# The second norm of a two-layer attention and experts kernel: its root by a power on GpSimd, its shift stored ahead, four pairs of rows loaded beside the experts

## The chip, the cores and the metric

One core of a Trainium2 chip runs the whole program in one launch. The metric is the device time of that launch in microseconds (us), a median over several runs.

## The reference

The input is x of 16 batches x 256 tokens x 256 features. Four units follow one another, each adding to x: an attention over a context (unit 0), self-attention with a top-2 mixture of eight small experts (unit 1), an attention over context and x jointly (unit 2, "joint"), and a full block (unit 3). Only the end of unit 3 and its sum with x matter here:

```python
h = layernorm(x + o, g1, b1)                    # o: causal attention
w = top2_shares(softmax(h @ wg))
h1 = gelu(einsum('bsd,edf->ebsf', h, w1) + bb1)
y = einsum('ebsf,efd->ebsd', h1, w2) + bb2
moe = einsum('ebsd,bse->bsd', y, w)
block = layernorm(h + moe, g2, b2)              # rsqrt(v + 1e-5) * g2 + b2
x = x + tanh(g_ffn[1]) * block
```

The x of the last line is the x after unit 2. With g = tanh(g_ffn[1]), the result is x + g*b2 + (normalised rows) * (g*g2).

## The kernel before

Four phases run one after the other, with a barrier of all engines between the blocks of each.

**Attention phase** (`attention_phase`). 64 jobs (unit, batch), in order of unit, flow through an order of steps that a planner (`orders`) writes out once, from the costs in `STAGES` and the needs in `job_steps`. Each engine, and the SP queue of DMAs, walks its own list `ORDER[engine]` strictly in order. A step of the SP list that waits for a semaphore holds all DMAs behind it, and a step of GpSimd (POOL) that waits holds all GpSimd work behind it. In unit 2, PROJ (PE, then DVE at L1251) completes x in a buffer `xs` (ring of seven); STOREX (L801) writes it to the DRAM tensor `x3`. Rings of three `o` buffers hold the heads' outputs. LNP (L1052, L1054) is the root of the norms in this phase: on GpSimd, an addition of EPS and a power of -0.5, both of 128x2 elements.

**Routing** (`route`) sorts the 8192 (token, choice) rows by expert, on DVE and PE at half clock, while SP and ScalarE load 17 MB of expert weights. **Experts** (`run_experts`) first has a block in which only SP acts (some semaphore counts and the wait for the weights, L1515 to L1522), then a block of 71 tiles of 128 rows: GpSimd gathers the rows of `h_normed` by an indirect DMA (L1535), PE turns them (L1571) and multiplies, GpSimd scatters the results into `expert_rows`, called `y_d` (L1543).

**The last stage** (`combine`) takes two batches at a time: 8 pairs, in a ring of 4 sets of buffers, as a hardware loop of two turns. Per pair SP loads h (512 KB), x (512 KB) and the two experts' rows y (1 MB) (L1718 to L1720). GpSimd adds b2 to x (L1731), when all three loads of the pair are there. DVE adds the experts' rows to h by their shares (L1777, eight instructions), takes mean and variance (L467, L470), the root by a guess in integers and three Newton steps (L439 to L452, twelve instructions of 128x4), and the shift (L1781). ScalarE normalises (L1751, four instructions); DVE multiplies by g2 and adds x (`add_residual`, L1766 and L1769), one pair behind; ScalarE issues two stores of 256 KB (L1743). The order on DVE is:

```python
for q in ring:
    ...                       # rows, moments, root, shift of pair q
    if q:
        add_residual(q - 1)
add_residual(RING - 1)
```

A block ahead of it loads g2 and b2 and multiplies them by g (L1696 to L1707).

Of the kernel before, what the change touches and what calls it, by code (L numbers as in the profile page):

```python
# [6 lines left out]
F32 = mybir.dt.float32  # L7
BF16 = mybir.dt.bfloat16
I32 = mybir.dt.int32
# [28 lines left out]
NEWTON = 3  # L38
# [36 lines left out]
def kv_at(u, b, src=0):  # L75
# [14 lines left out]
    "BPROJ": [("pool", 1.27)],  # L90
# [37 lines left out]
def heads_read(u, b):  # L128

    return [("FIN" if u < 2 else "PROJ", u, b, 0)] if u < 3 else [("HT", u, b, 0), ("STOREX", u, b, 0)]  # L130


def job_steps(u, b):
# [36 lines left out]
    x = add("LOADX", 0, ("STOREX", u - 1, b, 0) if u else None, (("STOREX" if old[0] < 3 else "PROJ"), *old, 0) if old else None)  # L170
# [184 lines left out]
BPROJ_AT = counted(of_kind("pool", "BPROJ"))  # L355
HNS_AT = counted(of_kind("dve", "HNS"))
# [38 lines left out]

class Chain:
# [36 lines left out]
RSQRT_GUESS = 0x5F3759DF  # L433
COMBINE_STEPS = 120


def root_guess(dve, s, var, out, v):

    s.done(dve.tensor_scalar(v, var, EPS, None, ALU.add))  # L439
    s.wait()  # L440
    s.done(dve.tensor_scalar(out.bitcast(I32), v.bitcast(I32), 1, None, ALU.logical_shift_right))  # L441
    s.wait()
    s.done(dve.tensor_scalar(out.bitcast(I32), out.bitcast(I32), -1.0, float(RSQRT_GUESS), ALU.mult, ALU.add))  # L443


def root_step(dve, s, out, v, w):

    s.done(dve.tensor_tensor(w, out, out, ALU.mult))  # L448
    s.wait()
    s.done(dve.scalar_tensor_tensor(out=w, in0=w, scalar=-0.5, in1=v, op0=ALU.mult, op1=ALU.mult))  # L450
    s.wait()
    s.done(dve.scalar_tensor_tensor(out=out, in0=w, scalar=1.5, in1=out, op0=ALU.add, op1=ALU.mult))  # L452


def inverse_root(dve, s, var, out, v, w):

    root_guess(dve, s, var, out, v)
    s.wait()
    for _ in range(NEWTON):
        root_step(dve, s, out, v, w)  # L460
        s.wait()


def norm_moments(dve, s, src, stats, mv, rstd, root_v, root_w, n):

    for t in range(n):
        s.done(dve.bn_stats(stats[:, t, :], src[:, t, :]))  # L467
    s.wait_alone()
    for t in range(n):
# [1342 lines left out]
```

## Time and profile before

| | us |
|---|---|
| median of 3 runs (2614.16 to 2621.49) | 2621.05 |
| the profiled execution's own time | 2617.61 |
| its span in the profile | 2615.9 |

The times in the rows are us from the start of the span. The span lies in the profiled execution's own time; 1.7 us lie around it. Over the whole span PE is busy 87%, DVE 64%, ScalarE 52%, GpSimd 37%, but these are averages over the four phases: after 2499 us PE does nothing at all. A change in one phase has to be read from that phase's rows.

### The profile page before, as it was taken

The numbers are of one execution on the slowest core, as the hardware profiler recorded it, in microseconds if no ns is written. First come the engines' busy times: TensorE is split into PE (matmuls) and PEld (weight loads), VectorE is DVE, ScalarE is ACT, GpSimd is POOL, SyncE is SP. The second block draws the span as 40 slices with busy tenths as digits, with TensorE's granted clock in tenths as the row PEclk, the third lists the DMA queues.
The fourth block names the chain that finished last, engine by engine and source line by source line (L and its number), as shares of the span: only waits on it lengthen the run. The fifth ranks groups of instructions, "written<-read, shape, count | busy, mean of one in ns | idle before, by whom it ended". The sixth has DMA issues, their size and how long they took to land. (4 is left out here: it accounts for less than half of the span.)

```text
span 2615.9 us, 52259 instructions
## 1 busy us (share of the span) xinstructions
PE 2282.1 (87%) x17492; PEld 1575.9 (60%) x17493; DVE 1686.8 (64%) x4481; ACT 1362.3 (52%) x2398; POOL 978.5 (37%) x1850
## 2 busy tenths in 40 slices
PE   2889999899999999999999999899848999999910
PEld 1445555555455556666666666666538999999910
DVE  4878886676767666777767668767563444443458
ACT  3889863454336346777777777767601222222211
POOL 5555412213122225333322247878602333333321
PEclk7999998999899999999999999999958999999965
DMA  7878623315134245544455445555180111111144
GB/s 216 206 192 208 148 67 82 88 38 122 30 88 95 65 99 135 116 116 113 112 118 120 107 116 109 122 133 129 42 277 27 34 36 37 36 36 32 35 173 156
DMA packets 209839, 275.49 MB, mean 105 GB/s; under 512 B 32606, under 2 KB 156489, under 8 KB 203370
## 3 DMA queue, kind: packets, MB, share of 16 engines
q1 hardware_dynamic: 196074, 242.38, 37.3%
q0 software_dynamic: 6912, 17.97, 2.2%
q10 hardware_dynamic: 6656, 12.58, 1.3%
q8 instruction: 116, 1.90, 0.3%
q14 instruction: 81, 0.66, 0.1%
HBM read 193.12 MB, written 80.64 MB: 105 GB/s over the span
## 5 line engine op out<-in xcount | busy, mean ns | idle before, releaser
L1035 ACT ACTIVATE ex<-t_ps 128x512 f32<-128x512 f32 (+1 forms) x1280 | 685.7, 579 | 203.0 <-PE t_ps L941 157.9
L1183 DVE TENSOR_REDUCE mx<-s_ps 128x2 f32<-128x512 f32 (+1 forms) x1024 | 659.9, 683 | 197.2 <-PE s_ps L912 125.2
L941 PE MATMUL t_ps<-qs,ks 123*128 123x256 bf16 x2048 | 355.5, 277 | 8.7 <-ACT ex L1035 3.7
L964 PE MATMUL pv_ps<-ex,va 128*17 128x256 f32 (+1 forms) x5120 | 318.1, 374 | 1.3 <-POOL ex L1087 1.3
L1029 ACT ACTIVATE qs<-tr_ps 27x2048 bf16<-27x2048 bf16 x128 | 239.2, 1869 | 108.3 <-PE tr_ps L925 105.5
L882 PE MATMUL pre_ps<-wexp,xt 128*128 128x512 f32 x512 | 270.5, 634 | 3.1 <-DVE moe L1242 2.2
L941 PEld LDWEIGHTS t_ps<-qs,ks 123*128 123x128 bf16 x2048 | 176.9, 98 | 156.1 <-ACT ex L1035 68.2
L1582 PEld LDWEIGHTS x_up_ps<-x_rows_t,x_wnow 128*128 128x128 f32 x2272 | 266.4, 193 | 5.3 <-issue 0.9
L1582 PE MATMUL x_up_ps<-x_rows_t,x_wnow 128*128 128x128 f32 x2272 | 267.0, 276 | 1.1 <-DVE x_pre L1645 0.7
L1592 PE MATMUL x_y_ps<-wdn,x_act 128*128 x1136 | 257.1, 379 | 0.7 <-DVE x_y L1653 0.7
L1612 ACT ACTIVATE x_rows_t<-x_rt_ps 128x256 f32<-128x256 f32 x72 | 27.6, 383 | 436.7 <-PE x_rt_ps L1571 436.7
L1592 PEld LDWEIGHTS x_y_ps<-wdn,x_act 128*128 128x128 f32 x1136 | 210.3, 190 | 26.8 <-issue 1.1
L1095 POOL TENSOR_SCALAR mp<-mx 128x16 bf16<-128x16 f32 x128 | 34.3, 268 | 512.2 <-DVE mx L1183 492.9
L918 PE MATMUL s_ps<-ks,qs 99*128 99x256 bf16 (+1 forms) x1024 | 186.6, 284 | 36.2 <-DVE mx L1183 24.7
L964 PEld LDWEIGHTS pv_ps<-ex,va 128*17 128x17 f32 x5120 | 124.8, 97 | 139.3 <-issue 49.9
L1176 DVE CUSTOM_DVE_ANT_0 s_ps<-s_ps,late 128x128 f32<-128x128 f32 (+1 forms) x512 | 166.8, 388 | 45.4 <-PE s_ps L915 45.2
L912 PE MATMUL s_ps<-ks,qs 96*128 96x256 bf16 x1024 | 180.0, 274 | 15.0 <-DVE mx L1183 8.5
L1640 DVE COPY x_wnow<-wup 128x1024 f32 x144 | 98.9, 688 | 144.9 <-issue 82.9
L1242 DVE SCALAR_TENSOR_TENSOR moe<-pre_ps,comb,moe 128x256 f32<-128x256 f32 x256 | 123.4, 482 | 91.2 <-PE pre_ps L882 84.3
L1039 ACT ACTIVATE ot<-pv_ps 128x256 f32<-128x256 f32 x256 | 99.8, 390 | 133.2 <-PE pv_ps L964 130.8
L918 PEld LDWEIGHTS s_ps<-ks,qs 99*128 99x128 bf16 (+1 forms) x1024 | 86.4, 100 | 126.6 <-DVE mx L1183 73.3
L1078 POOL TENSOR_TENSOR ak<-ak,pk 128x512 f32<-128x512 f32 x64 | 74.7, 1167 | 218.8 <-ACT pk L1016 112.5
(248 smaller groups left out, 3739.7 us busy)
## 6 DMA issues: line engine op xcount, KB each, us to landing
q_parts<-pq SPq DMA_DIRECT2D x128, 192.0 KB
qs<-q_parts SPq DMA_DIRECT2D x64, 384.0 KB, 4.9
qs<-q_parts SPq DMA_DIRECT2D x192, 128.0 KB, 5.8
k_parts<-pk SPq DMA_DIRECT2D x96, 192.0 KB
ks<-k_parts SPq DMA_DIRECT2D x96, 192.0 KB
ks<-k_parts SPq DMA_DIRECT2D x288, 64.0 KB
ks<-ctx_k_parts SPq DMA_DIRECT2D x64, 192.0 KB
ks<-ctx_k_parts SPq DMA_DIRECT2D x192, 64.0 KB
```

Source lines behind the costliest of these rows:

```text
L882: end_pre(step, pe.matmul(bank[:, :], xt_now[:, turn, t * P:(t + 1) * P], wexp[:, turn, e:e + 2, :].rearrange("p e n -> p (e n)"), start=t ...
L912: last = pe.matmul(dst[:, r * T:(r + 1) * T], q(src), key(r)[0:rows, h, :], start=True, stop=True)
L918: last = pe.matmul(dst[:, t * T:(t + 1) * T], q(t), key(0)[0:rows, h, :], start=True, stop=True)
L941: last = pe.matmul(dst[:, t * T:(t + 1) * T], key[0:ROWS, h, t * P:(t + 1) * P], qs[q_at][0:ROWS, h, :], start=True, stop=True)
L964: last = pe.matmul(pv_ps[i * VS:i * VS + VW, q0:T], val[:, t, k * QH + i, :], e, start=r == 0 and t == 0, stop=r == srcs - 1 and t == NT - ...
L1029: act.activation(qs[q_at][PRODUCTS:ROWS, k * HG:(k + 1) * HG, :], tr_b[PRODUCTS:ROWS, 0:T].unsqueeze(1).broadcast_to([ROWS - PRODUCTS, HG, ...
L1035: act.activation(ex[:, n % EXPS, 0:w], t_ps[n % 2][:, 0:w], ACT.Exp).then_inc(t_read, 1)
L1176: last = dve.tensor_tensor_reduce(out=seen, in0=seen, in1=late[:, 2 * P - w:2 * P], scale=1.0, scalar=FUTURE, op0=ALU.add, op1=ALU.max, ac ...
L1183: dve.tensor_reduce(dst, s_ps[n % S_BANKS][:, :].rearrange("p (a b) -> p a b", a=dst.shape[-1]), AX.X, ALU.max).then_inc(s_read, 1)
L1242: last = dve.scalar_tensor_tensor(out=moe[r][:, t, :], in0=bank[:, n * D:(n + 1) * D], scalar=comb[r][:, t, e + n:e + n + 1], in1=moe[r][: ...
L1582: last = pe.matmul(up_ps[h][:, g * P:(g + 1) * P], wnow[k][h][:, c, g * P:(g + 1) * P], rows_t[:, c, :], start=c == 0, stop=c == DC - 1)
L1592: last = pe.matmul(y_ps[:, 0:D], act_t[k][h][:, g, :], wdn[:, bass.ds(x, 1), f, :].rearrange("p e n -> p (e n)"), start=f == 0, stop=f == ...
```

## The change

1. **Attention phase.** In unit 2 a new step XB on GpSimd adds g*b2 to the finished x of the job (128x512) into the job's `o` buffer, and a new step STOREB on SP stores that to a new DRAM tensor `x3_shifted` (16 stores of 256 KB). The load into an `xs` buffer that held a joint job now also waits for its XB, and DVE's first write into an `o` buffer (step OT) for the STOREB of the joint job that had it. b2 is loaded and multiplied in the setup block, by one DMA and one DVE instruction.
2. **Experts.** In the block in which only SP acts, SP issues the loads of h and shifted x of pairs 0 to 3 (eight DMAs of 512 KB) after its wait for the weights. Their buffers are now allotted ahead of the experts' weights.
3. **Last stage.** One block without a loop. SP loads g2, the y of four pairs, then per further pair h, x and y when its buffers are stored. GpSimd's addition of b2 is gone; GpSimd takes the root instead, by an addition of EPS and a power of -0.5, both of 128x4. The DVE's twelve root instructions are gone, the shares are read in place (no copies), and DVE's order is rows and moments of pair n, `add_residual(n - 1)`, shift of pair n. The output of a pair is one store of 512 KB.

The diff, cut to its core:

```diff
 def heads_read(u, b):
-    return [("FIN" if u < 2 else "PROJ", u, b, 0)] if u < 3 else [("HT", u, b, 0), ("STOREX", u, b, 0)]
+    return {0: [("FIN", u, b, 0)], 1: [("FIN", u, b, 0)], 2: [("STOREB", u, b, 0)], 3: [("HT", u, b, 0), ("STOREX", u, b, 0)]}[u]
...
+        if u == 2:
+            add("STOREB", 0, add("XB", 0, s))
...
+                    elif name == "STOREB":
+                        sp.wait_ge(x_shifted, XB_AT[("XB", u, b, 0)] + 1)
+                        sp.dma_start(xb_d[b], o[o_at][:, :, :]).then_inc(b_stored[o_at], 16)
...
+                    elif name == "XB":
+                        wait_copied(pool, ("PROJ", u, b, 0))
+                        pool.tensor_tensor(o[uses_before("o", (u, b))[1]][:, :, :], xs[x_at][:, :, :], b2[:, :].unsqueeze(1).broadcast_to([P, NT, D]), ALU.add).then_inc(x_shifted, 1)
...
                 sp.wait_ge(a["w_loaded"], 16 * (3 * E + 2))
+                for q in range(RING):
+                    sp.dma_start(flat_pair(a["c_h"][q]), a["hn_d"][2 * q:2 * q + 2].rearrange("b p t n -> p b (t n)")).then_inc(a["c_loaded"][q], 16)
+                    sp.dma_start(flat_pair(a["c_x"][q]), a["xb_d"][2 * q:2 * q + 2].rearrange("b p t n -> p b (t n)")).then_inc(a["c_loaded"][q], 16)
...
+            @block.sync
+            def _(sp):
                 sp.dma_start(g2[:, :], a["ln2_g"].partition_broadcast(P)).then_inc(small, 16)
+                for n in range(PAIRS):
+                    q = n % RING
+                    if n >= RING:
+                        sp.wait_ge(out_stored[q], 16 * (n // RING))
+                        sp.dma_start(flat_pair(hb[q]), ...).then_inc(head_loaded[q], 16)
+                        sp.dma_start(flat_pair(xb[q]), ...).then_inc(head_loaded[q], 16)
+                    sp.dma_start(flat_pair(yb[q]), ...).then_inc(y_loaded[q], 16)
...
+            @block.gpsimd
+            def _(pool):
+                pool.memset(power[:, :], -0.5).then_inc(consts, 1)
+                pool.wait_ge(consts, 1)
+                for n in range(PAIRS):
+                    q = n % RING
+                    pool.wait_ge(moments, n + 1)
+                    pool.tensor_scalar(rstd[q][:, :], mv[q][:, :, 1], EPS, None, ALU.add).then_inc(pool_step, 1)
+                    pool.wait_ge(pool_step, n + 1)
+                    pool.tensor_tensor(rstd[q][:, :], rstd[q][:, :], power[:, :], ALU.pow).then_inc(rooted, 1)
...
+                for n in range(PAIRS):
+                    add_rows(n)
+                    if n:
+                        add_residual(n - 1)
+                    shift_rows(n)
+                add_residual(PAIRS - 1)
```

The planner's order is the same as before up to the end of unit 2 but for the two new steps. On GpSimd in unit 2, now (each row an instruction: line, operation, what it writes and reads; `mp` and `mr` hold parts of the maxima, `va` the values, `o1` is an `o` buffer):

```order
L1077 CAST mp2<-mr0 128x2x8
L1079 TENSOR_TENSOR mp2<-mr0,mp2 128x2x8
L1048 COPY va0<-ctx0 128x32x16
L1082 TENSOR_TENSOR o1<-xs6,b2 128x512
L1072 TENSOR_SCALAR mp3<-mx2 128x2x8
L1073 TENSOR_SCALAR mr1<-mx2 128x16
L1075 TENSOR_TENSOR mr1<-mr1,mp3 128x16
```

The row L1082 is the new XB (line numbers are those of the changed kernel); the rows around it stood next to each other before. What stands behind it is the second half of the maxima of the next job's attention.

On SP, at the entry to the experts and to the last stage, now:

```order
L1499 UNCONDITIONAL_BRANCH
L1510 DMA c_h<-h_normed 128x2x512
L1511 DMA c_x<-x_shifted 128x2x512
...
L1498 UNCONDITIONAL_BRANCH
L1680 UNCONDITIONAL_BRANCH
L1682 DMA c_g<-in_L_ffn_g 128x256
L1689 DMA c_y<-expert_rows 128x2x1024 x4
L1687 DMA c_h<-h_normed 128x2x512
```

Between the branches L1499 and L1498 (the block in which only SP acts) stand four such couples, eight DMAs; before, nothing stood there. In the last stage the four loads of y now come right behind g2, without h and x.

On DVE in the last stage, one pair, before and now (before, the three rows from L448 to L452 come three times, and the register instructions between the rows are left out):

```order
L467 BN_STATS c_stats<-c_h 128x6 x4
...
L470 BN_AGGR c_mv<-c_stats 128x2 x4
...
L439 TENSOR_SCALAR c_root_v<-c_mv 128x4
...
L448 TENSOR_TENSOR c_root_w<-c_rstd 128x4
...
L1781 SCALAR_TENSOR_TENSOR c_shift<-c_mv,c_rstd 128x4
...
L1766 TENSOR_TENSOR c_h<-c_h,c_g 128x1024
...
L1769 TENSOR_TENSOR c_h<-c_h,c_x 128x1024
```

```order
L1720 BN_STATS c_stats<-c_h 128x6 x4
L1723 BN_AGGR c_mv<-c_stats 128x2 x4
L1737 TENSOR_TENSOR c_h<-c_h,c_g 128x1024
L1739 TENSOR_TENSOR c_h<-c_h,c_x 128x1024
L1731 SCALAR_TENSOR_TENSOR c_shift<-c_mv,c_rstd 128x4
L1716 SCALAR_TENSOR_TENSOR c_h<-c_y,share_of,c_h 128x256 x8
```

The root rows are gone from DVE, and the shift has moved behind the two instructions of `add_residual` of the pair before. In unit 3 the planner writes many steps in another order than before, from the second job on, with the same steps in all.

## Rows read from the trace of the kernel before

**Rows 1.** Busy time by stretch: the attention phase, the last stage

```profile
0.00:1903.00 1903.00, 1734.40 (x13808) 1060.28 (x13809) 1345.27 (x3767) 1231.55 (x2150) 778.67 (x1550) 0.96 0.48 115
2499.00:2616.00 117.00, 0.00 (x0) 0.00 (x0) 89.85 (x258) 16.60 (x32) 19.45 (x9) 0.50 0.50 182
```

**Rows 2.** DVE in time, one undisturbed pair: start, us, line, operation

```profile
2589.32 3.37 DVE L1777 SCALAR_TENSOR_TENSOR c_h<-c_y,c_share,c_h 128x256 f32<-128x256 f32 x8
...
2594.69 0.17 DVE L439 TENSOR_SCALAR c_root_v<-c_mv 128x4 f32<-128x4 f32 x1
...
2597.07 0.16 DVE L1781 SCALAR_TENSOR_TENSOR c_shift<-c_mv,c_rstd 128x4 f32<-128x4 f32 x1
2597.15 1.22 DVE L1766 TENSOR_TENSOR c_h<-c_h,c_g 128x1024 f32<-128x1024 f32 x1
...
2599.55 3.37 DVE L1777 SCALAR_TENSOR_TENSOR c_h<-c_y,c_share,c_h 128x256 f32<-128x256 f32 x8
```

**Rows 3.** DVE and GpSimd in time, a pair with an addition of b2

```profile
2576.05 5.47 DVE L1777 SCALAR_TENSOR_TENSOR c_h<-c_y,c_share,c_h 128x256 f32<-128x256 f32 x8
...
2577.01 2.52 POOL L1731 TENSOR_TENSOR c_x<-c_x,c_b 128x1024 f32<-128x1024 f32 x1 [12.63 <-DMA c_y<-expert_rows]
```

**Rows 4.** The first and the last work of the last stage, in time

```profile
2503.52 0.35 SPq L1696 DMA_DIRECT2D c_g<-in_L_ffn_g  x1
...
2509.82 0.41 SPq L1718 DMA_DIRECT2D c_h<-h_normed  x1
...
2510.96 0.37 SPq L1720 DMA_DIRECT2D c_y<-expert_rows  x1
...
2517.70 5.45 DVE L1777 SCALAR_TENSOR_TENSOR c_h<-c_y,c_share,c_h 128x256 f32<-128x256 f32 x8 [7.80 <-DMA c_y<-expert_rows]
...
2607.51 2.08 ACT L1751 ACTIVATE c_h<-c_h,c_shift,c_rstd 128x256 f32<-128x256 f32 x4 [8.16 <-DVE c_shift L1781]
...
2611.03 1.22 DVE L1769 TENSOR_TENSOR c_h<-c_h,c_x 128x1024 f32<-128x1024 f32 x1
```

**Rows 5.** Busy time by stretch, while SP's first loads of the last stage land

```profile
2515.00:2530.00 15.00, 0.00 (x0) 0.00 (x0) 11.63 (x32) 2.07 (x4) 6.63 (x3) 0.50 1.04 398
```

**Rows 6.** A norm's root on GpSimd, at the program's start, in time

```profile
27.44 0.25 DVE L1132 BATCH_NORM_AGGREGATE mv<-stats 128x2 f32<-128x6 f32 x2
27.78 0.24 POOL L1052 TENSOR_SCALAR rstd<-mv 128x2 f32<-128x2 f32 x1 [20.42 <-DVE mv L1132]
28.11 0.73 POOL L1054 TENSOR_TENSOR rstd<-rstd,power 128x2 f32<-128x2 f32 x1
```

**Rows 7.** The entry to the experts, in time

```profile
1971.00 0.19 POOL L1533 COPY x_row_now<-row_of 128x1 int32<-128x1 int32 x1 [67.06 <-SPq L1524]
1971.94 2.51 DVE L1640 COPY x_wnow<-wup 128x1024 f32 x4 [2.35 <-issue]
1972.17 1.80 POOL L1535 DMA_INDIRECT x_rows<-h_normed,x_row_now  x1 [0.98 <-POOL x_row_now L1533]
1973.98 0.50 POOL L1533 COPY x_row_now<-row_of 128x1 int32<-128x1 int32 x1
...
1975.82 0.69 PE L1571 MATMUL x_rt_ps<-ident,x_rows 128*128 128x128 f32 x2 [7.71 <-DMA x_rows<-h_normed,x_row_now]
```

**Rows 8.** SP's queue in time: issues without a wait, and one behind eight others

```profile
0.82 0.41 SPq L575 DMA_DIRECT2D lens<-in_itok_Bx  x1
...
5.75 0.38 SPq L586 DMA_DIRECT2D bexp<-in_L_ffn_b_experts  x1
...
2516.05 1.02 SPq L1718 DMA_DIRECT2D c_h<-h_normed  x1
```

**Rows 9.** Waits in unit 2 (1000 to 1520 us): us in total, times, longest

```profile
POOL mp L1095 <- DVE mx L1183: 190.5, 27, 12.1
...
SPq L751 <- DMA x<-xs: 23.9, 14, 2.4
```

**Rows 10.** GpSimd's addition in unit 2: ns least/median/most, first and last start

```profile
L1105 POOL TENSOR_TENSOR xs<-xs,bproj x16: 1260/1268/1374, 848.5 to 1337.2; 128x512 f32<-128x512 f32 x16
```

More of the change, by code:

```diff
@@ L169, in job_steps @@
     old = JOBS[j - NX] if j >= NX else None
-    x = add("LOADX", 0, ("STOREX", u - 1, b, 0) if u else None, (("STOREX" if old[0] < 3 else "PROJ"), *old, 0) if old else None)
+    x = add("LOADX", 0, ("STOREX", u - 1, b, 0) if u else None, (("STOREX" if old[0] < 3 else "PROJ"), *old, 0) if old else None, ("XB", *old, 0) if old and old[0] == 2 else None)
     values = []
@@ L430, in stand @@
         self.eng.sem_inc(self.passed, 1)
[L433 to L469, printed above, removed]
-        s.done(dve.bn_aggr(mv[:, t, :], stats[:, t, :]))
-    s.wait()
-    inverse_root(dve, s, mv[:, :, 1], rstd[:, :], root_v[:, :], root_w[:, :])
 def build(nc, x, ctx_in, itok, g_xattn, g_ffn, key_b, w0_qkv, b0_qkv, w0_gate, b0_gate, w0_exp, b0_exp,
@@ new lines, in _, with add_rows @@
+                s = Chain(dve, step)
+                rows = g2[:, :].unsqueeze(1).broadcast_to([P, QT, D])
+                def add_rows(n):
+                    q = n % RING
+                    dve.wait_ge(head_loaded[q], 32 * (n // RING + 1))
+                    dve.wait_ge(y_loaded[q], 16 * (n // RING + 1))
+                    for j in range(TOPK):
+                        for t in range(QT):
+                            s.done(dve.scalar_tensor_tensor(out=hb[q][:, t, :], in0=yb[q][:, t * TOPK + j, :], scalar=share_of[:, n * QT + t, j:j + 1],
+                                                            in1=hb[q][:, t, :], op0=ALU.mult, op1=ALU.add))
+                        s.wait()
+                    for t in range(QT):
+                        s.done(dve.bn_stats(stats[q][:, t, :], hb[q][:, t, :]))
+                    s.wait()
+                    for t in range(QT):
+                        last = dve.bn_aggr(mv[q][:, t, :], stats[q][:, t, :])
+                        if t < QT - 1:
+                            s.done(last)
+                    last.then_inc(moments, 1)
@@ new lines, in shift_rows, with add_residual @@
+                def shift_rows(n):
+                    q = n % RING
+                    dve.wait_ge(rooted, n + 1)
+                    dve.scalar_tensor_tensor(out=shift[q][:, :], in0=mv[q][:, :, 0], scalar=-1.0, in1=rstd[q][:, :],
+                                             op0=ALU.mult, op1=ALU.mult).then_inc(shifted, 1)
+                def add_residual(n):
+                    q = n % RING
+                    dve.wait_ge(normed, n + 1)
+                    s.done(dve.tensor_tensor(hb[q][:, :, :], hb[q][:, :, :], rows, ALU.mult))
+                    s.wait()
+                    dve.tensor_tensor(hb[q][:, :, :], hb[q][:, :, :], xb[q][:, :, :], ALU.add).then_inc(finished, 1)
@@ L1736, in _ @@
+                dve.wait_ge(small, 16)
+                dve.tensor_scalar(g2[:, :], g2[:, :], tanh_g[:, 3:4], None, ALU.mult).then_inc(row_ready, 1)
+                dve.wait_ge(row_ready, 1)
+                for n in range(PAIRS):
[4 more added lines that the diff above has]
+                add_residual(PAIRS - 1)
             @block.scalar
             def _(act):
[L1738 to L1755 removed]
@@ new lines, in store @@
+                def store(n):
+                    act.wait_ge(finished, n + 1)
+                    act.dma_start(a["out"][2 * n:2 * n + 2].rearrange("b (t p) d -> p (b t) d", p=P), hb[n % RING][:, :, :]).then_inc(out_stored[n % RING], 16)
+                for n in range(PAIRS):
+                    q = n % RING
+                    act.wait_ge(shifted, n + 1)
+                    for t in range(QT):
+                        last = act.activation(hb[q][:, t, :], hb[q][:, t, :], ACT.Identity, bias=shift[q][:, t:t + 1], scale=rstd[q][:, t:t + 1])
+                    last.then_inc(normed, 1)
+                    if n:
+                        store(n - 1)
```

125 lines of the change are left out of this document (37 added, 88 removed).

## The prediction

> **What bounds the kernel now.** I read the busy time by stretch first: in the attention phase PE is busy 1734 of 1903 us, while in the last 117 us PE has no instruction and DVE is busy 89.9 us [rows 1]. So a change to the norm at the end must be priced on DVE's path in the last stage, and whatever it adds ahead of that on the paths of PE and SP. Then I read the last stage in time. DVE starts at 2517.70, when the first pair's rows have landed, and its last instruction ends at 2611.03 + 1.22 = 2612.25 [rows 4]: 94.6 us with hardly a gap. The span ends 3.65 us later, after the last store. One undisturbed pair takes 2599.55 - 2589.32 = 10.23 us [rows 2]: rows and moments 5.37 (to 2594.69), root and shift 2.46 (to 2597.15), residual of the pair before 2.40. Eight such pairs are 81.8 us, so 12.7 us of the 94.6 are something else. Most of it is seen in [rows 3]: the eight row instructions of a pair take 5.47 us instead of 3.37 where GpSimd's 2.52 us addition of b2 runs beside them. DVE stands still for 2.1 us, about as long as that addition runs.
>
> **The last stage, start.** SP's first load is issued at 2503.52, but h only at 2509.82 and y at 2510.96, behind a block of their own for g2 and b2; DVE starts 7.88 us after the issue of h, with 2 MB to land [rows 4]. At 398 GB/s [rows 5] 1 MB is 2.63 us. Now y goes out right behind g2, near 2504.0, and is alone: 7.88 - 2.63 = 5.25 us later is 2509.2. If y needed as long as it did behind h and x (2517.70 - 2510.96 = 6.74) it would be 2510.7. I take 2509.3, the nearer count of bytes: **-8.4 us** (bounds -7.0 and -8.5).
>
> **The last stage, body.** Three things leave DVE: the root (2.38 of the 2.46 us), GpSimd's long additions, and the copies of shares. What comes is a wait for GpSimd. For a pair behind the first, count from the end of its moments:
> - DVE goes on at once with the first residual instruction (1.22 us and a step's wait: 1.25). GpSimd hears of the moments after 0.09 us and would need 0.24 for EPS and, 0.09 later, 0.73 for a power of 128x2 [rows 6].
> - But DVE and GpSimd hold each other up. In [rows 7] a GpSimd copy that takes 0.19 us alone takes 0.50 from 1973.98, and ends at 1974.48, as DVE's copies end (1971.94 + 2.51 = 1974.45); in [rows 3] it is GpSimd that has the way and DVE that waits. The residual's instructions read two tensors of SBUF, as the row instructions of [rows 3] do. So I count the addition of EPS as held to the first residual instruction's end, 1.25, and done at 1.30. DVE's second residual instruction, held 0.05 by that, is there before the power, and ends at 2.52.
> - The power is held to 2.52. No row has a power of 128x4: 0.73 is the low bound (the time is all setup), 1.46 the high one (twice the elements). EPS of 128x2 takes 0.24, so about 0.5 of the 0.73 is the power itself; I take 1.0, between. Its first 0.1 us or so passes while it waits: done near 3.40, and with a hop of 0.05 and the shift (0.16 and its step) DVE starts the next pair at 3.65.
>
> A pair is then 5.37 + 3.65 = 9.02 us instead of 10.23. The first pair has no residual to wait behind: 5.37 + 1.65 = 7.02. After the last shift ScalarE's four instructions (2.08 us, [rows 4]) now stand open, since no residual runs beside them: with hops 2.18, then the last residual, 2.47. Sum: 7.02 + 7 x 9.02 + 4.65 = 74.8 us against 94.6: **-19.8 us**.
>
> The Trainium skill (SBUF — State Buffer, Who interferes with whom) says that VectorE and GpSimd share a pair of ports as an exclusive lock, which a VectorE instruction with two SBUF inputs takes against a GpSimd instruction that reads SBUF. It speaks against putting the root where the residual runs, and by it the pair is the 9.02 us above; without it, it would be 7.97 us (the first rival).
>
> The ring of four sets does not bind: the first pair is finished at 7.0 + 5.4 + 2.5 = 14.9 us after DVE's start, ScalarE issues its store only behind its work for the second pair, near 18.2, it lands by 21.5 (3.3 us, less than the 3.65 from DVE's end to the span's), and 7.9 us later, at 29.4, pair 4 is loaded; DVE wants it at 7.0 + 3 x 9.02 = 34.1. The end behind the last residual stays at 3.65 us: one issue less, one store twice as large, **0**.
>
> **The entry to the experts.** Here the change adds. All engines wait at the end of the block in which SP acts (GpSimd's first instruction there is released by SP, [rows 7]), and eight DMA issues now stand in it. Without waits, ten issues go out in 5.75 - 0.82 = 4.93 us [rows 8], 0.49 each: **+4.0 us** (3.3 at 0.41 each; 8.2 at 1.02 each, the price behind eight others in [rows 8]). Nothing covers it: the gather, PE's turn and the first multiplication follow in a chain.
> The 4 MB need 10.5 us at 398 GB/s, and 2.6 us stand on top of the bytes (5.25 - 2.63, above). Issued from about 1970.6 on, just ahead of GpSimd's release at 1971.00, they are all in near 1983.7, while the first gather, which reaches PE at 1975.82 now [rows 7], would do so at 1979.8. If it shares the engines with them it is late by about 1 us; if it waits until all are in, by 3.9. I take **+1.0** (bounds 0 and 3.9). Later gathers run a tile ahead and hide.
> The Trainium skill (DMA: Bandwidth & Descriptors, Queues, rings and completion order) says that a DMA engine goes round the queues that have work, packet by packet. By it the gather's queue shares, which is the 1 us; strict order would be 3.9. No row of this trace has a gather beside such loads.
>
> **The attention phase.** Setup gets one DMA issue (0.49) and one DVE instruction: **+0.5** (0 to 0.9). XB costs GpSimd 16 x 1.27 us [rows 10]. In unit 2 GpSimd waits 190.5 us in 27 waits, 7 us each, for DVE's maxima [rows 9], and XB stands right ahead of such a wait: free. STOREB waits 1.3 us for XB on SP, with LOADX behind it; but LOADX already waits for the store before it, 23.9 us in 14 waits, 1.7 each [rows 9]: free, and the load is needed seven jobs later. If that cover were gone, it would be 16 x 1.3 = 21 us. The last XB falls into unit 3, where GpSimd masks each head's weights: up to 1.3. Unit 3's steps stand in another order; no row can tell its sign. I take **+1.0** for both, and -4 to +4 as bounds: what two or three stalls of 1.3 us would give or take.
>
> **Sum.** -8.4 - 19.8 + 4.0 + 1.0 + 0.5 + 1.0 = **-21.7 us**. From the profiled execution's own 2617.6 that is 2595.9; the median of the runs shown is 3.4 us above that execution, and on it 2621.05 - 21.7 = 2599.4. I predict **2599 us**. About 0.3% (7.9 us) is what a measurement of this kernel can tell from no change.
>
> **The rivals.**
> - *The root hides whole.* If GpSimd's two small instructions slip between or beside the residual's, a pair is 5.37 + 2.40 + 0.20 = 7.97 us, and 7 x 1.05 = 7.3 us more are won: 2592. For it: they touch SBUF for a moment. Against it: [rows 3, 7]. Chance 0.20.
> - *The early loads are dear.* Issues at 1.02 us (+4.2) and a gather behind all 4 MB (+2.9): 2606. For it: SP's issues slow down behind eight others in [rows 8]. Against it: those had 5 MB ahead of them, these at most 3.5. Chance 0.13.
> - *XB blocks GpSimd's list* (the slower side). If PROJ completes later than the planner thinks, XB holds up the next maxima, those the transposes and PE. It decides where this costs over (21.7 + 7.9) / 16 = 1.9 us per joint job beyond GpSimd's slack; at 3 us per job the kernel would take 2621 - 21.7 + 48 = 2647. Against it: the 7 us of waiting per half job. Chance 0.04.
> - *No difference.* Both high bounds at the experts' entry (+7.1), a power of 1.46 us (+3.7) and the high bound of the attention phase (+3) leave 7.9 us of gain, 2613: the edge of what can be told. Chance 0.05.
> - The forecast itself has 0.58.
>
> **The numbers.** Faster by over 0.3% are the forecast, the first two rivals: 0.58 + 0.20 + 0.13 = 0.91. Within 0.3%: 0.05. Slower: 0.04. The range reaches down to the hidden root with the attention phase at its low bound and part of the 3.4 us between runs (2592 - 4 - 2 = 2586), and up to the dear loads with the attention phase high (2606 + 3, and 1 for a longer power: 2610).
>
> **What would show it.** DVE's pair in the last stage near 9.0 us with a wait of about 1 us ahead of the shift; GpSimd's power as long as 1.0 us or more, starting or ending at the end of the second residual instruction; row instructions of 3.4 us in all eight pairs; DVE's start some 6 us after g2's issue; SP's eight issues ahead of the experts in some 4 us, with GpSimd released right behind them; an attention phase within 4 us of 1903. A pair of 8.0 us would refute the held root, one over 9.5 the power's price; an attention phase off by 10 us would make the whole prediction wrong, whatever the last stage does.

## The result, and the profile after

The changed kernel takes **2595.37 us** (median of 5 runs, 2590.12 to 2600.12), the kernel before beside it 2620.65; the ratio is 0.9915, with a 95% interval from 0.9899 to 0.9931. That is faster by 0.85%, inside the range and 3.6 us under the predicted 2599. The profiled execution has a span of 2593.6 us against 2615.9: 22.3 us less, where the sum of my terms was 21.7. The terms themselves were not all that good: the profile has 2.6 us more than forecast for the gather and 1.4 more for the start of the last stage, 2.5 less for its body and 3.0 less ahead of the experts, and these nearly took each other away. Measured once more (below), the two medians lay 20.6 us apart (2618.96 and 2598.40).

Busy time by stretch (PE, PEld, DVE, ScalarE, GpSimd, then the granted clock, the DMA share and GB/s), answering to [rows 1]:

```profile
0.00:1903.00 1903.00, 1731.92 (x13808) 1061.03 (x13809) 1346.11 (x3768) 1230.93 (x2150) 800.30 (x1570) 0.97 0.49 117
1970.00:1982.00 12.00, 0.00 (x0) 0.00 (x0) 2.51 (x4) 0.00 (x0) 3.50 (x4) 0.50 1.03 364
2510.00:2593.60 83.60, 0.00 (x0) 0.00 (x0) 60.98 (x153) 16.60 (x32) 23.03 (x17) 0.50 0.56 202
```

The attention phase is nearly the same but for GpSimd's 21.6 us more (the sixteen XB are 20.2 of them). The last stage has 61 us of DVE left of 90. In between stand 12 us in which PE does nothing while the DMA engines are full. The last stage in time, its start and then one pair, with DVE, GpSimd and ScalarE (answers to [rows 2 to 4]):

```profile
2510.69 0.34 SPq L1682 DMA_DIRECT2D c_g<-in_L_ffn_g  x1
...
2517.91 1.27 DVE L1716 SCALAR_TENSOR_TENSOR c_h<-c_y,share_of,c_h 128x256 f32<-128x256 f32 x3 [2.37 <-DMA c_y<-expert_rows]
...
2523.32 0.23 POOL L1700 TENSOR_SCALAR c_rstd<-c_mv 128x4 f32<-128x4 f32 x1 [12.53 <-DVE c_mv L1723]
2523.64 1.05 POOL L1702 TENSOR_TENSOR c_rstd<-c_rstd,c_power 128x4 f32<-128x4 f32 x1
...
2524.81 3.38 DVE L1716 SCALAR_TENSOR_TENSOR c_h<-c_y,share_of,c_h 128x256 f32<-128x256 f32 x8
...
2529.96 1.19 DVE L1737 TENSOR_TENSOR c_h<-c_h,c_g 128x1024 f32<-128x1024 f32 x1
2530.13 1.12 POOL L1700 TENSOR_SCALAR c_rstd<-c_mv 128x4 f32<-128x4 f32 x1 [5.44 <-DVE c_mv L1723]
2531.19 1.22 DVE L1739 TENSOR_TENSOR c_h<-c_h,c_x 128x1024 f32<-128x1024 f32 x1
2531.34 1.97 POOL L1702 TENSOR_TENSOR c_rstd<-c_rstd,c_power 128x4 f32<-128x4 f32 x1
2533.34 0.16 DVE L1731 SCALAR_TENSOR_TENSOR c_shift<-c_mv,c_rstd 128x4 f32<-128x4 f32 x1 [0.93 <-POOL c_rstd L1702]
```

Read GpSimd's two instructions twice. Behind the first pair, with DVE idle, they take 0.23 and 1.05 us. Behind the second, beside the residual, they take 1.12 and 1.97. The addition of EPS starts in DVE's first residual instruction and ends at 2531.25, with it (2529.96 + 1.19 = 2531.15). The power starts inside the second and ends 0.9 us behind that one's end (2532.41). DVE then stands idle for 0.93 us. The next pair starts at 2533.42, so a pair is 8.61 us (the first starts at 2524.81), and from the first addition to the last residual's end DVE needs 2590.18 - 2517.91 = 72.3 us against 94.6. The entry to the experts (answers to [rows 7, 8]):

```profile
1969.00 0.37 SPq L1510 DMA_DIRECT2D c_h<-h_normed  x1
...
1972.70 0.50 SPq L1511 DMA_DIRECT2D c_x<-x_shifted  x1
...
1973.71 0.19 POOL L1522 COPY x_row_now<-row_of 128x1 int32<-128x1 int32 x1 [71.05 <-SPq L1513]
1974.83 1.84 POOL L1524 DMA_INDIRECT x_rows<-h_normed,x_row_now  x1 [0.93 <-POOL x_row_now L1522]
...
1982.13 0.69 PE L1560 MATMUL x_rt_ps<-ident,x_rows 128*128 128x128 f32 x2 [15.55 <-DMA x_rows<-h_normed,x_row_now]
```

DVE ends `row_of` at 1968.06, and GpSimd's first copy starts 5.65 us later (1.41 before): eight issues stand between. From there to PE's first turn it is 8.42 us (4.82 before): the gather's rows land late. In unit 2 GpSimd's waits, longest sums first, now read (us, times, longest; answer to [rows 9]):

```profile
POOL o L1082 <- DVE xs L1234: 111.0, 15, 10.1
...
POOL mp L1072 <- DVE mx L1163: 71.9, 27, 4.3
```

The 190.5 us that GpSimd waited for DVE's maxima are split: 111.0 now stand ahead of XB (for the finished x), 71.9 behind it. Together they are 7.6 us less, while XB adds 16 x 1.26 = 20.2 us of work; so these sums alone don't show that XB is free. The length of unit 2 does. From the first start to the last start of its sixteen projections, in the kernel before, in the changed one and in the run e7 below, which has no XB:

```profile
L1251 DVE SCALAR_TENSOR_TENSOR xs<-pre_ps,tanh_g,xs x16: 750/751/752, 1042.2 to 1565.7; 128x512 f32<-128x512 f32 x16
...
L1234 DVE SCALAR_TENSOR_TENSOR xs<-pre_ps,tanh_g,xs x16: 749/750/752, 1037.1 to 1560.6; 128x512 f32<-128x512 f32 x16
...
L1227 DVE SCALAR_TENSOR_TENSOR xs<-pre_ps,tanh_g,xs x16: 749/751/752, 1040.1 to 1563.6; 128x512 f32<-128x512 f32 x16
```

That is 523.5 us three times, and 523.3 to 523.5 in 13 of the 14 profiles of this case (525.0 in e9): XB costs nothing in unit 2.

### The profile page after: what moved, and what is told of

Read it like the earlier page. It is cut to its first block and busy times, and to the rows that moved or that the text cites. A ratio compares the mean times of both kernels' runs of the same rounds, so it can differ in the third digit from the quotient of the medians.

```text
span 2593.6 us, 51898 instructions
## 1 busy us (share of the span) xinstructions
PE 2280.5 (88%) x17492; PEld 1577.5 (61%) x17493; DVE 1658.5 (64%) x4377; ACT 1358.8 (52%) x2398; POOL 1004.2 (39%) x1875
```

## The account by stage

The executions of one kernel lie up to 18 us apart (the kernel before, 2607.49 to 2625.58 in one set of runs), and the profiles show where. `row_of`, the last result of the routing, is ready at 1968.06 in the changed kernel; over the 14 profiles of this case, whose code ahead of that point hardly differs, it is ready between 1957.9 and 1975.5 us. What follows repeats within a few tenths of a us, but for the experts (521.6 to 523.1). So I compare, beside the medians, the time from `row_of`'s end to the end of the span, split at five points: GpSimd's first copy, PE's first turn, the issue of the last scatter, DVE's first addition in the last stage and the end of its last instruction. All us:

```
                        row_of  ->copy ->turn experts ->add   body  tail | behind row_of | median
before                  1969.6    1.4    4.8   522.2  19.7    94.5   3.7 |     646.3     | 2620.65
changed                 1968.1    5.6    8.4   523.1  12.7    72.3   3.4 |     625.5     | 2595.37
changed again           1975.5    5.7    8.5   522.4  12.6    72.3   3.5 |     625.0     | 2598.40
e1 spread               1969.5    1.8    4.7   522.2  12.5    72.3   3.5 |     617.1     | 2592.22
e1b spread again        1967.1    1.8    4.8   522.3  12.5    72.3   3.4 |     617.1     | 2587.58
e2 beside               1970.1    1.8    7.3   522.8  12.5    72.3   3.4 |     620.1     | 2591.97
e3 no early loads       1971.7    1.8    4.8   522.4  15.2    72.3   3.4 |     619.9     | 2594.78
e4 Newton on DVE        1968.0    6.0    8.4   521.9  12.6    81.0   3.4 |     633.3     | 2603.47
e5 no EPS               1974.4    6.0    8.2   522.2  12.7    66.3   3.5 |     618.7     | 2594.66
e6 b2 in last stage     1968.8    5.6    8.4   521.6  14.6    88.9   3.5 |     642.6     | 2614.15
e7 no b2                1969.1    5.6    8.4   521.9  12.5    71.9   3.5 |     623.6     | 2594.13
e8 shift behind         1957.9    6.2    8.2   521.9  12.6    67.8   3.4 |     620.1     | 2591.96
e8b and y early         1967.5    5.6    7.8   522.3  13.0    65.1   3.4 |     617.3     | 2586.58
e9 all                  1964.9    1.8    4.8   523.1  10.9    65.3   3.5 |     609.4     | 2579.58
```

## The experiments

All start from the changed kernel.

**The early loads.** Does the entry's loss come from SP's issues, from the gather's delay, or from something else? The first run moves the eight loads to where the experts' tiles cover them:

```diff
         with nc.Block() as block:
+            @block.sync
+            def _(sp):
+                for q in range(RING):
+                    sp.wait_ge(y_done, 16 + 8 * q)
+                    sp.dma_start(... c_h[q] ...)
+                    sp.wait_ge(y_done, 20 + 8 * q)
+                    sp.dma_start(... c_x[q] ...)
```

> The eight loads of h and of the shifted x move from the block ahead of the experts into the experts' own block, one behind every fourth tile from the sixteenth on. My account of the entry to the experts: the changed kernel lost 4.24 us there because no engine enters the block before SyncE has issued eight DMAs, 3.6 us because the first gather's packets lie behind 4 MB of loads, and 0.85 us in the first tile; all 8.7 us should come back and the last stage stay as it is: span 2584.9 us against 2593.6 (about 2586.6 by the timed runs). Rival: each load of 512 KB (1.3 us at 398 GB/s) holds up the gather or scatter of the tile it falls into, and up to 1.3 us of each shows: span 2585 to 2595. Other rival: the entry's loss has nothing to do with these loads, span 2593.6.

Measured: 617.1 us behind `row_of`, 8.5 less, 7.5 of them at the entry. The first copy is 1.8 us behind `row_of` (1.4 in the kernel before) and the turn 4.7 behind that, as before the change:

```profile
1971.32 0.19 POOL L1527 COPY x_row_now<-row_of 128x1 int32<-128x1 int32 x1 [67.90 <-POOLq L1498]
...
1976.06 0.69 PE L1565 MATMUL x_rt_ps<-ident,x_rows 128*128 128x128 f32 x2 [8.02 <-DMA x_rows<-h_normed,x_row_now]
```

The loads cost nothing where they now stand: the experts take 522.2 us, as before. I had also charged 0.85 us of a slower first tile to them, since the changed kernel's experts took 523.1. That was wrong: seven other profiles with the same early loads have 521.6 to 522.4, and the run that has none of them at the entry and everything else, e9, has 523.1. It belongs to the execution.

The second run drops the waits and issues the loads at the start of the experts' block, beside the first gathers:

> The eight loads are issued at the start of the experts' own block, beside GpSimd's first gathers, instead of in the block ahead of it. This takes the wait for SyncE's eight issues away (4.24 us, measured as row_of's end to GpSimd's first copy, 1.41 to 5.65) and leaves the transfers where they were. If the gather stood behind what had been issued before it, only the one or two loads issued earlier by then hold it up now (1.3 us each): first copy to first turn of PE 6 to 7.5 us against 8.42, span 2588 to 2589. If queues with work take packets in turn, first copy to first turn is 5 to 6 us, span 2586 to 2587. If the gather has to stand behind all 4 MB wherever it is issued, it is 10 us or more and the span 2592 to 2594, little better than the change.

Measured 620.1 us, and 7.3 us from the first copy to the first turn. SP's queue and GpSimd in time, then PE's turn:

```profile
1971.77 0.37 SPq L1514 DMA_DIRECT2D c_h<-h_normed  x1
1972.19 0.47 SPq L1515 DMA_DIRECT2D c_x<-x_shifted  x1
1972.71 2.90 SPq L1514 DMA_DIRECT2D c_h<-h_normed  x1
1975.66 0.47 SPq L1515 DMA_DIRECT2D c_x<-x_shifted  x1
...
1973.00 1.84 POOL L1527 DMA_INDIRECT x_rows<-h_normed,x_row_now  x1 [0.93 <-POOL x_row_now L1525]
...
1979.18 0.69 PE L1563 MATMUL x_rt_ps<-ident,x_rows 128*128 128x128 f32 x2 [10.57 <-DMA x_rows<-h_normed,x_row_now]
```

The wait for SP's issues is gone (3.9 of the 4.2 us). The delay of the gather is not: when its issue ends at 1974.84, three loads (1.57 MB) have been issued, and its rows reach PE 4.34 us later, against 1.78 in the first run (1974.28 to 1976.06) and 1982.13 - 1976.67 = 5.46 in the changed kernel, where all eight had been issued and some 1.9 MB had still to land (364 GB/s from 1970 on). More ahead, later. What the DMA engines moved meanwhile, by queue (q1 is SP's queue, q0 GpSimd's; packets, MB, share of the 16 engines), shows more. The changed kernel from 1976.67 to 1980.00 (one row), then to 1982.13 (two rows):

```profile
q1 hardware_dynamic: 671, 1.30, 104.9%
...
q1 hardware_dynamic: 307, 0.58, 75.6%
q0 software_dynamic: 76, 0.22, 27.9%
```

For 3.3 us behind its issue the gather moves no packet at all, while SP's loads move 1.30 MB. Then packets of both queues go side by side, and at PE's turn only 0.03 MB of the loads is left. In the first run, with no load beside it, its first packet comes 0.5 us behind the issue. Here, in the second, it comes 1.2 us behind (at 1976.0), 45 of its 48 packets are through by 1977.0, when 1.06 of the three loads' 1.57 MB have moved; the last three packets come only from 1978.2 on, and at PE's turn 1.86 MB of loads have moved. So it is not a strict order of issues, but PE waits for the last packet, and the price is close to that of one.

The third run has no early loads:

```diff
-                for q in range(RING):
-                    sp.dma_start(... c_h[q] ...)
-                    sp.dma_start(... c_x[q] ...)
...
                     if n >= RING:
                         sp.wait_ge(out_stored[q], 16 * (n // RING))
-                        sp.dma_start(... hb[q] ...)
-                        sp.dma_start(... xb[q] ...)
+                    sp.dma_start(... hb[q] ...)
+                    sp.dma_start(... xb[q] ...)
```

> No early loads: h and the shifted x of the first four pairs are loaded in the last stage, ahead of their pair's y, as for the later pairs. The entry to the experts should be that of the kernel before (8.7 us less), and the first addition of the last stage wait for 1 MB and two issues more, 2.6 to 3.6 us. Span 2593.6 - 8.7 + 3.1 = 2588.0 us (2586.5 to 2589.5), so the early loads cost more than they bring at this place. Rival: the early loads are what made the start of the last stage 7 us shorter; then it grows by 7.0 us again and the span is 2591.9.

Measured 619.9 us, 5.6 less than the changed kernel. DVE's first addition comes 2.5 us later, close to the 1 MB at 398 GB/s (2.6), and nothing else in the last stage moves. So at the place where the change put them, the early loads lose: they bring 2.5 us and cost 7.5. Of the 7.0 us that the change won at the start of the last stage, 4.5 are there without them; they come from dropping the block of its own.

**The root.** The next run gives it back to DVE:

```diff
+                    inverse_root(dve, s, mv[q][:, :, 1], rstd[q][:, :], root_v[:, :], root_w[:, :])
+                    dve.scalar_tensor_tensor(out=shift[q] ...).then_inc(shifted, 1)
...
-                    pool.tensor_scalar(rstd[q] ..., EPS, None, ALU.add)
-                    pool.tensor_tensor(rstd[q] ..., power[:, :], ALU.pow)
```

> The root goes back to VectorE (a guess and three Newton steps, twelve small instructions) and everything else of the change stays. Theory: GpSimd's power is worth what VectorE's root took less what is left of the wait: the pair goes from 8.61 us to 5.15 (additions, moments) + 2.4 (root, shift) + 2.45 (residual) = 10.0 us, the last stage's body from 72.3 to 72.3 + 7 x 1.4 + 1.1 = 83.2 us. Rival: the pair became shorter because GpSimd no longer adds the shift beside VectorE, and the root's place is worth little: body 72 to 76 us.

A pair is 10.11 us, and the body 81.0: the rival's 72 to 76 is out, the root on GpSimd is worth 1.5 us a pair. The body is 2.2 us under my number because I forgot the end: here the residual of pair 6 runs while ScalarE normalises pair 7, which in the changed kernel DVE waits out for 2.14 us. The DVE instructions that start two pairs, in time (the view ends within the second):

```profile
2534.78 3.37 DVE L1736 SCALAR_TENSOR_TENSOR c_h<-c_y,share_of,c_h 128x256 f32<-128x256 f32 x8
...
2544.89 1.27 DVE L1736 SCALAR_TENSOR_TENSOR c_h<-c_y,share_of,c_h 128x256 f32<-128x256 f32 x3
```

What holds GpSimd's two instructions? One of them is taken away:

```diff
-                    pool.tensor_scalar(rstd[q][:, :], mv[q][:, :, 1], EPS, None, ALU.add).then_inc(pool_step, 1)
-                    pool.wait_ge(pool_step, n + 1)
-                    pool.tensor_tensor(rstd[q][:, :], rstd[q][:, :], power[:, :], ALU.pow).then_inc(rooted, 1)
+                    pool.tensor_tensor(rstd[q][:, :], mv[q][:, :, 1], power[:, :], ALU.pow).then_inc(rooted, 1)
```

> GpSimd takes the power of the variance alone: the addition of EPS ahead of it is left out, and so is EPS in the result. In the changed kernel the addition takes 1.12 us and the power 1.98 us while VectorE multiplies and adds the residual (0.23 and 1.05 us alone). Theory A, the two instructions wait for each other's turn at the port, each for one of VectorE's: with one of them gone the power ends while the residual's second instruction still runs, VectorE's 0.93 us of idle time before the shift goes, pair 7.7 us, body 72.3 - 7 x 0.93 - 0.3 = 65.5 us. Theory B, the power cannot run at all while VectorE works on the residual and only starts behind it: then it ends no earlier, pair 8.4 to 8.6 us, body 70.5 to 72.3 us.

The body is 66.3 us, theory A. DVE and GpSimd in time:

```profile
2535.08 1.19 DVE L1735 TENSOR_TENSOR c_h<-c_h,c_g 128x1024 f32<-128x1024 f32 x1
2535.25 1.89 POOL L1700 TENSOR_TENSOR c_rstd<-c_mv,c_power 128x4 f32<-128x4 f32 x1 [5.43 <-DVE c_mv L1721]
2536.31 1.22 DVE L1737 TENSOR_TENSOR c_h<-c_h,c_x 128x1024 f32<-128x1024 f32 x1
2537.45 0.15 DVE L1729 SCALAR_TENSOR_TENSOR c_shift<-c_mv,c_rstd 128x4 f32<-128x4 f32 x1
```

The power starts inside the first residual instruction, and ends at 2537.14: 0.87 us behind that one's end and 0.39 us before the second one's. It is held by the instruction of DVE that is under way, not by the one that follows. In the changed kernel the addition of EPS is held by the first and the power by the second. Each of GpSimd's instructions pays for one of DVE's and then needs most of its own time; with both of them in the chain, the power's last 0.90 us come behind the residual, and that is the 0.93 us of idle time.

**The addition of b2.** It goes back into the last stage, on GpSimd behind the power:

```diff
...
                     pool.tensor_tensor(rstd[q][:, :], rstd[q][:, :], power[:, :], ALU.pow).then_inc(rooted, 1)
+                    pool.wait_ge(head_loaded[q], 32 * (n // RING + 1))
+                    pool.tensor_tensor(xb[q][:, :, :], xb[q][:, :, :], b2 ..., ALU.add).then_inc(x_ready, 1)
```

> The shift b2 is added in the last stage again: the joint jobs store no second copy, the last stage loads x itself, and GpSimd adds b2 to each pair's x behind the pair's power. In the kernel before, this addition took 2.52 us and stretched one of VectorE's additions from 0.48 to 2.57 us. Theory: it does so here, so that each pair takes 2.1 us more: body 72.3 + 8 x 2.1 = 89 us (two thirds of what the last stage gained came from taking this addition away). Rival: the root's and the residual's new order leave idle time in which the addition hides: body 72.3 + 8 x 0.9 = 80 us or less.

Measured: a body of 88.9 us, as the theory had it. In time:

```profile
2547.28 2.33 POOL L1699 TENSOR_TENSOR c_x<-c_x,c_b 128x1024 f32<-128x1024 f32 x1
2547.34 2.30 DVE L1728 SCALAR_TENSOR_TENSOR c_shift<-c_mv,c_rstd 128x4 f32<-128x4 f32 x1 [0.93 <-POOL c_rstd L1697]
2549.56 3.37 DVE L1713 SCALAR_TENSOR_TENSOR c_h<-c_y,share_of,c_h 128x256 f32<-128x256 f32 x8
```

DVE's shift, 0.16 us of work on 128x4, takes 2.30 us: it stands from its start to the end of GpSimd's addition. The pair becomes 2549.56 - 2538.82 = 10.74 us, 2.13 more. The Trainium skill (SBUF — State Buffer, Who interferes with whom) calls this an exclusive lock on a shared pair of ports; by it either engine waits out the other's instruction. The trace agrees both ways round: GpSimd's 0.23 us became 1.12, DVE's 0.16 became 2.30. Putting b2's addition back costs 16.7 us of body, putting the root back 8.7; that is more than the 22.3 that the change won, so the two don't simply add. No run puts both back. (The start is 1.9 us later too: b2 is loaded and multiplied ahead of the first pair.)

The other half of that question is what the addition costs in the attention phase:

> The shift b2 is left out altogether (the result lacks it): no addition and no second store in the joint jobs, x itself loaded in the last stage, no addition there. This prices what the change put into the attention phase. The last stage's body stays at 72.3 us. Theory: GpSimd's 16 additions of 1.1 to 1.3 us and 4.2 MB of stores hide there, so the time is that of the changed kernel, 2592 to 2596 us. Rival: they hold VectorE off and cost up to my bound of 4 us: 2589 to 2591 us. Executions of the same attention phase have so far ended between 1957.9 and 1971.7 us, so only the median of several runs can say anything.

The median is 2594.13 us, 21.8 under the kernel before beside it (2615.88). The changed kernel's two medians lie 25.3 and 20.6 under theirs, so the medians can't tell what b2 costs. Behind `row_of` it is 623.6 us, 1.9 and 1.3 less than in the changed kernel's two profiles, 0.4 of it in the body. Ahead of `row_of`, unit 2 is as long with XB as without (523.5 us, above).

Unit 3, from the last projection of unit 2 to the last start of its own sum (L1237), takes 326.3, 326.4 and 328.3 us in the three profiles with the old order (before, e6, e7) and 326.9 to 332.2, on average 329.5, in the eleven with the new one. That may be a price of some 2.5 us for the new order. But these lengths also go with the granted clock: where it was at the lower of its two levels for 14 us of the stretch they are 326.3 to 327.2 in both orders, and where for 24 or 25 us, 331.4 and 332.2. No run takes the two apart.

**A better order.** While GpSimd takes the root, DVE may do something else. It takes the shift of pair n-1 between the two halves of pair n's additions:

```diff
                     for j in range(TOPK):
+                        if j and n:
+                            shift_rows(n - 1)
                         for t in range(QT):
...
                     if n:
                         add_residual(n - 1)
-                    shift_rows(n)
+                shift_rows(PAIRS - 1)
                 add_residual(PAIRS - 1)
```

> VectorE takes the shift of pair n-1 not right behind its own moments but between the two halves of pair n's additions, so that GpSimd's power and ScalarE's normalization run while VectorE adds rows. Theory: the pair of 8.61 us is 5.15 (additions and moments) + 2.41 (residual) + 0.93 idle for the root + the shift; the idle 0.93 goes: pair 7.7 us, seven times, span 2593.6 - 6.5 = 2587.1 us. Rival: the lock of the port moves the loss: the power cannot be taken between the additions (each 0.42 us with VectorE's next one right behind), and comes so late that VectorE waits for it in the middle of the additions: pair 8.2 to 8.8 us, span 2590 to 2595.

```profile
2519.69 1.66 DVE L1718 SCALAR_TENSOR_TENSOR c_h<-c_y,share_of,c_h 128x256 f32<-128x256 f32 x4
2521.39 0.16 DVE L1733 SCALAR_TENSOR_TENSOR c_shift<-c_mv,c_rstd 128x4 f32<-128x4 f32 x1
...
2526.27 1.98 POOL L1702 TENSOR_TENSOR c_rstd<-c_rstd,c_power 128x4 f32<-128x4 f32 x1
...
2527.27 1.67 DVE L1718 SCALAR_TENSOR_TENSOR c_h<-c_y,share_of,c_h 128x256 f32<-128x256 f32 x4
...
2552.34 1.67 DVE L1718 SCALAR_TENSOR_TENSOR c_h<-c_y,share_of,c_h 128x256 f32<-128x256 f32 x4 [2.23 <-DMA c_y<-expert_rows]
...
2561.22 1.67 DVE L1718 SCALAR_TENSOR_TENSOR c_h<-c_y,share_of,c_h 128x256 f32<-128x256 f32 x4 [1.20 <-DMA c_y<-expert_rows]
```

The pair is 7.58 us, the root hidden whole and the additions no longer than before. But the body is 67.8 us, not the 65.8 that the expectation comes to: at this pace two pairs wait for y, 3.4 us in all. SP loads y only when the store of four pairs earlier has landed, though that store reads another buffer:

```diff
                     if n >= RING:
+                        sp.wait_ge(moments, n - RING + 1)
+                    sp.dma_start(flat_pair(yb[q]), ...)
+                    if n >= RING:
                         sp.wait_ge(out_stored[q], 16 * (n // RING))
...
-                    sp.dma_start(flat_pair(yb[q]), ...)
```

> As the run with the shift between the halves of the next pair's additions, and y of pair n+4 is loaded as soon as pair n has been added (it waited for pair n's store to land before, though that store doesn't read y). In the earlier run the pair was 7.58 us, 1.03 less than in the changed kernel, but VectorE waited 3.4 us for y of pairs 5 and 6 (2.23 and 1.20). Theory: these waits came only from the order of the loads; they go, body 67.8 - 3.4 = 64.4 us, and from row_of's end to the end of the span 620.1 - 3.4 = 616.7 us. Rival: at 7.58 us a pair the transfers (2 MB in and 0.5 MB out, 6.6 us at 398 GB/s, each load behind a landed store) have become the bound, and the waits come back at another place: body 66 to 68 us.

Measured: body 65.1 us; the waits for y are gone, and one of 0.86 us, for x of a late pair, is new. The theory holds but for that; the rival's 66 does not. Then all edits that paid, in one kernel:

> The edits that paid, together: early loads spread among the experts' tiles (8.4 us less), shift between the halves of the additions and y loaded early (body 64.4 us instead of 72.3), and g2 loaded and scaled behind the first y (0.5 us less, from the 0.39 us of its issue and 0.1 MB). From row_of's end to the end of the span 625.5 - 8.4 - 7.9 - 0.5 = 608.7 us; by the median 2595.4 - 16.8 = 2578.6 us (2575 to 2582). Rival: a gain at the entry and one in the last stage do not add, since TensorE's work in the experts takes what it takes: 2585 us or more.

The median is **2579.58 us** (2576.04 to 2581.44), 0.9854 of the kernel before [0.9838, 0.9871], and 609.4 us behind `row_of` (0.7 over the forecast). The gains add. DVE's first addition comes 1.8 us sooner than in the changed kernel, more than the 0.5 expected. The price was less g2's issue than what its load does to y behind it. The first issue of y and DVE's first addition, with no such load ahead (e9), and with two, g2 and b2 (e6):

```profile
2500.14 0.36 SPq L1691 DMA_DIRECT2D c_y<-expert_rows  x1
...
2505.52 3.38 DVE L1726 SCALAR_TENSOR_TENSOR c_h<-c_y,share_of,c_h 128x256 f32<-128x256 f32 x8 [12.12 <-DMA c_y<-expert_rows]
...
2510.82 3.03 SPq L1683 DMA_DIRECT2D c_y<-expert_rows  x4
...
2519.01 3.38 DVE L1713 SCALAR_TENSOR_TENSOR c_h<-c_y,share_of,c_h 128x256 f32<-128x256 f32 x8 [2.09 <-DMA c_y<-expert_rows]
```

From issue to addition it is 5.4 us in e9, 6.8 (2511.08 to 2517.91) behind g2 in the changed kernel and 8.2 behind g2 and b2 in e6: 1.4 us for each 128 KB, which at 398 GB/s would be 0.3. The first 3 us from y's issue, in the changed kernel and in e9 (the last two numbers are the DMA share and GB/s):

```profile
2511.08:2514.08 3.00, 0.00 (x0) 0.00 (x0) 0.00 (x0) 0.00 (x0) 0.00 (x0) 0.50 0.68 93
...
2500.14:2503.14 3.00, 0.00 (x0) 0.00 (x0) 0.00 (x0) 0.00 (x0) 0.10 (x1) 0.50 0.60 173
```

With g2 among the loads the engines are a little busier and move about half as much. The one wait of 0.83 us for x stays. This is the best kernel of the study.

**Can single profiles be trusted?** The medians disagreed with the account: e1's was only 3.2 us under the changed kernel's, while its profile had 8.5 us less behind `row_of`. Both were run again side by side.

> The changed kernel as it is, beside the next run on the same chip. The attention phase and the routing, whose code hardly differs between the kernels so far, ended between 1957.9 and 1974.4 us in their profiles, while what follows agreed within some tenths of a us. Expected: from row_of's end to the end of the span 625.5 us again (within 1 us), the median 2592 to 2597 us, and executions up to 10 us apart. If the stretch behind row_of moves by more than 1 us, the account of the single profiles is not good enough.

> The kernel with the eight early loads spread among the experts' tiles once more, beside the changed kernel on the same chip. In its profile 8.4 us had come back behind row_of, while its median lay only 3.2 us under the changed kernel's 2595.4. Theory: the stretch behind row_of is 617.1 us again, the difference of the medians is the scatter of the attention phase, and the two medians now lie 5 to 12 us apart. Rival: the spread loads cost something elsewhere, in the attention phase or between executions, and the medians differ by 3 us or less again.

Behind `row_of` 625.0 and 617.1 us, medians 2598.40 and 2587.58: now 10.8 us apart. The profile was right and the median of five too coarse for 8 us. Over all executions of both pairs of runs the medians are 2597.7 and 2589.2 (11 each), 8.5 apart.

## Why the prediction was right, and where it was off

1. **Start of the last stage, -8.4 forecast, -7.0 measured** (g2's issue to DVE's first addition, 14.18 to 7.22 us). The mechanism is right and the size is the smaller of my bounds. I counted y as alone, 5.25 us from its issue; it took 6.8. The count of bytes was not at fault: with y first, in e9, it takes 5.4. What I had at nothing is the load of g2 ahead of it: 1.4 us.
2. **Body, -19.8 forecast, -22.3 measured.** All three parts are there: eight times 3.38 us of additions with no stretched one, the root gone from DVE, and an idle time ahead of the shift. The rows and moments are 5.15 us and not 5.37 (0.15 of the difference is a wait of DVE ahead of the moments that is gone); the held root is 3.46 us and not 3.65. The power of 128x4 takes 1.05 us by itself, against 1.0 taken between 0.73 and 1.46. That GpSimd's instructions are held, one by one, was the deciding step, and the runs without EPS and with b2 show it. The first rival (hidden root, 7.97 us a pair) is refuted at 8.61 in this order of the work, and true in another one (7.58).
3. **Entry to the experts, SP's issues: +4.0 forecast, +4.2 measured.** All eight took 4.2 us from first to last; that they stand open was right. 3.9 us of it goes with them: in e3, without any load there, the first copy still comes 1.8 us behind `row_of` against 1.4 before.
4. **Entry, the gather: +1.0 forecast, +3.6 measured. This step failed.** I let the gather share the engines with the loads from its issue on. For 3.3 us it moved no packet, then it shared, and it was in when the loads were, close to my bound of 3.9. The Trainium skill (DMA: Bandwidth & Descriptors, Queues, rings and completion order) has an engine go round the queues that have work, packet by packet. The last 2.1 us agree with that (76 packets of GpSimd's queue among 307 of SP's); the 3.3 us ahead of them I had not counted. Why GpSimd's queue moved nothing for so long, the runs don't show. The second rival's half (a gather behind everything) was nearly true, its other half (issues at 1.02 us) not.
5. **Attention phase and setup, +1.5 forecast.** `row_of` came 1.5 us sooner in this pair of profiles, which says nothing beside a scatter of 17.6 us. XB is free in unit 2, which is 523.5 us long with it and without. Unit 3 may have become some 2.5 us longer, inside my bounds of -4 to +4; that can't be told from the granted clock's part.
6. **End, 0 forecast, -0.2 measured.**

So the forecast was right for the reasons given in its two large terms. That it came within 0.6 us of the span's difference is luck: the gather's 2.6 us, the start's 1.4 and 0.9 us in the experts were made up by the body's 2.5 us and by where the attention phase happened to end (3.0 us sooner than forecast).

## What to carry to other kernels

An early load is free only where nothing urgent is queued behind it: in a block that all engines leave together each issue is on the path, and the first urgent transfer behind it waits for most of its bytes. A row spread to all partitions delays it by more than its bytes say. When a small job moves to GpSimd beside a busy DVE, count for each of its instructions the rest of the DVE instruction under way and then most of its own time, and give DVE other work until it is done. Where executions scatter, find the point in the profile behind which they agree and compare from there.

## What was not expected of the hardware

- A gather issued behind 4 MB of SP's loads is in only when they are: 5.46 us from the end of its issue to PE's turn, 4.34 behind three loads, 1.78 with none. Its first packet moves 3.3, 1.2 and 0.5 us behind the issue.
- A load of a row to all partitions (g2, b2; 128 KB) holds up the load behind it by 1.4 us: y took 5.4, 6.8 and 8.2 us from its issue to DVE's first addition with none, one and two of them ahead.
- A DVE instruction of 0.16 us took 2.30 us beside GpSimd's addition of 2.33 us; a GpSimd instruction of 0.23 us took 1.12 us beside DVE's of 1.19.
- SP's third load in the run with loads beside the gathers took 2.90 us to issue (0.47 its neighbours), in the stretch in which GpSimd issued the first gather (1973.00 to 1974.84). No run takes this apart.
- The same attention and routing code ended up to 17.6 us apart between executions (1957.9 and 1975.5 us), while the 520 us of experts behind it agreed within 1.6. Of the 17.6 us, 13.0 are there when unit 2's first projection starts (1029.8 to 1042.8). That start goes with the granted clock: between 100 and 1030 us the profiles have it at the lower of its two levels for 58 to 82 us (1.2 against 2.4 GHz; PEclk read in stretches of 10 us and summed); with 58 us (e8) the projection starts at 1029.8, with 82 (e5) at 1042.6, and over all 14 the correlation is 0.94. What moves the clock was not looked into.
